# A tuned FFN-and-attention kernel: a new order of one tile's work on all five engines

## What is computed

```
xn  = layernorm(x)
# linear attention, 16 heads of 16
q, k, v = split(xn @ W_qkv.T + b_qkv);  q, k = elu(q) + 1, elu(k) + 1
kv  = sum_n k_n v_n ;  k1 = sum_n k_n
att = (q @ kv) / max(q . k1, 1e-6)
att = layernorm(att @ W_proj.T + b_proj) * gamma + beta + xn
# feed-forward with ternary weights, scales per output
h   = silu(xn @ w1.T * s1) * (xn @ w2.T * s2)       # 256 -> 1024
h   = gelu(h @ h1.T * t1)                           # 1024 -> 1024
h   = gelu(h @ h2.T * t2)                           # 1024 -> 1024
out = x + att + h @ w3.T * s3                       # 1024 -> 256
```

## Time and profile before

| what | value |
|---|---|
| median of 3 runs | 1734.03 us (1733.47 to 1736.09) |
| the profiled execution | 1730.4 us |
| its span in the profile | 1728.5 us |
| granted clock of TensorE, mean | 0.978 |
| busy: PE / DVE / ACT / POOL | 1562.2 / 1213.1 / 969.2 / 501.1 us |
| one tile of the loop | 102.1 us |
| from the start of the first tile's gate groups to that of the second's | 165.5 us |

### The profile page before, as it was taken

How to read it: one execution, slowest core, us unless ns; L and a number is a source line. 1 busy time by engine, 2 the same in 40 slices (tenths; PEclk the granted TensorE clock), 3 DMA queues, 4 the chain that set the end, 5 groups by cost and what they waited for, 6 DMA issues and landing times.

```text
span 1728.5 us, 32973 instructions
## 1 busy us (share of the span) xinstructions
PE 1562.2 (90%) x10956; PEld 1438.9 (83%) x10956; DVE 1213.1 (70%) x2083; ACT 969.2 (56%) x1745; POOL 501.1 (29%) x573
## 2 busy tenths in 40 slices
PE   6474999999999999999999999999999999999997
PEld 4474888888988888898888989888898888889897
DVE  3574686876868677685867768686685867768585
ACT  3243465655647465565755656565564656556463
POOL 3221150422314133240512314052231413323040
PEclk8697999999999999999999999999999999999999
DMA  6885255371735536173462626437172553717343
GB/s 229 316 325 187 92 205 182 109 255 51 263 106 182 195 112 234 57 252 138 140 232 91 228 89 227 162 116 254 52 260 98 195 186 113 243 43 261 129 159 132
DMA packets 84962, 298.15 MB, mean 172 GB/s; under 512 B 7232, under 2 KB 44224, under 8 KB 59584
## 3 DMA queue, kind: packets, MB, share of 16 engines
q0 software_dynamic: 37152, 238.04, 39.3%
q1 hardware_dynamic: 47344, 58.49, 10.0%
q10 hardware_dynamic: 432, 1.18, 0.2%
HBM read 280.91 MB, written 23.07 MB: 176 GB/s over the span
## 4 chain that ended last, share of the span: by engine, by line
PE 43%; DVE 20%; issue 16%; ACT 10%; DMA 4%; POOL 3%; DVEq 1%; SPq 0%; ACTq 0%; POOLq 0%
PE ps L830 19%; PE ps L859 7%; PE ps L804 5%; DVE partial_sums L1284 4%; PE ps L709 4%; DVE operands_a L1261 4%; PE ps L710 3%; PE ps L711 3%; DVE values_a L1253 3%; DVE operands_b L1261 2%; ACT operands_a L1008 2%; ACT values_out L1033 2%; ACT gate_ring L971 2%; POOL values_a L609 2%; DMA weight_set<-in_w_ffn 2%
## 5 line engine op out<-in xcount | busy, mean ns | idle before, releaser
L830 PE MATMUL ps<-operands_a,hidden_weights 128*128 128x256 f32 x5376 | 755.1, 286 | 61.6 <-DVE operands_a L1261 36.7
L830 PEld LDWEIGHTS ps<-operands_a,hidden_weights 128*128 128x128 f32 x5376 | 686.4, 191 | 88.1 <-DVE operands_a L1261 49.4
L830 PE MATMUL ps<-operands_b,hidden_weights 128*128 128x256 f32 x1792 | 298.2, 288 | 56.9 <-DVE partial_sums L1284 42.1
L830 PEld LDWEIGHTS ps<-operands_b,hidden_weights 128*128 128x128 f32 x1792 | 247.3, 191 | 69.6 <-DVE partial_sums L1284 45.8
L1284 DVE TENSOR_TENSOR partial_sums<-partial_sums,ps 128x512 f32<-128x512 f32 x320 | 214.3, 681 | 126.1 <-PE ps L830 125.5
L1261 DVE TENSOR_TENSOR operands_a<-values_a,operands_a 128x512 fp32r<-128x512 f32 x336 | 272.2, 825 | 41.9 <-ACT operands_a L996 22.3
L625 POOL DMA_DIRECT2D hidden_weights<-weight_blocks x252 | 138.0, 548 | 523.4 <-PE ps L830 510.6
L804 PE MATMUL ps<-xnT,w_ffn 128*128 128x512 f32 x1024 | 252.2, 401 | 15.3 <-DVE values_a L1253 15.3
L804 PEld LDWEIGHTS ps<-xnT,w_ffn 128*128 128x128 f32 x1024 | 191.7, 190 | 59.9 <-DVE values_a L1253 16.2
L1033 ACT ACTIVATE values_out<-partial_sums,vectors 128x256 f32<-128x256 f32 x192 | 86.9, 500 | 181.1 <-DVE partial_sums L1284 179.6
L1008 ACT ACTIVATE operands_a<-values_a 128x512 fp32r<-128x512 f32 x192 | 120.9, 630 | 107.8 <-POOL values_a L619 49.3
(11 more groups left out here) (112 smaller groups left out, 2083.2 us busy)
## 6 DMA issues: line engine op xcount, KB each, us to landing
hidden_weights<-weight_blocks POOLq DMA_DIRECT2D x192, 1024.0 KB, 5.6
hidden_weights<-weight_blocks POOLq DMA_DIRECT2D x64, 512.0 KB, 3.8
raw_weights<-weight_blocks SPq DMA_DIRECT2D x48, 272.0 KB, 5.5
x<-in_H SPq DMA_DIRECT2D x16, 512.0 KB, 5.1
weight_set<-in_w_ffn SPq DMA_DIRECT2D x16, 512.0 KB, 10.7
out_dram<-acc SPq DMA_DIRECT2D x32, 256.0 KB, 2.2
weight_blocks<-in_w_ffn SPq DMA_DIRECT2D x12, 512.0 KB, 10.6
weight_blocks<-weight_set SPq DMA_DIRECT2D x4, 1536.0 KB, 7.2
```

The source lines that it names most:

```text
L830: r = mm(bank[:, m * HT:(m + 1) * HT], ring_weights[:, place, 2 * g + j, m * P:(m + 1) * P], as_used(buf[:, j, slot[block_of_b], part, :]) ...
```

## The change

No operation is added or taken from the steady tile; the same instructions are issued in another order, and the waits are moved with them. The parts:

- **Product loops.** The chunk pair (g) is now the outer loop, then the part, then the bank's half (m), then the chunk.
- **Banks.** Set 0 and 2 use banks 4, 5, 0 in place of 0, 1, 4; sets 1 and 3 use 1, 2, 3 in place of 5, 2, 3. Only the wait conditions of the first products change.
- **PE.** The two `kv_sums` and the two first `apply_kv` come later among the gate groups; the attention projection (`proj_step`) comes after set 1's P1 and P6 instead of before them; in the first tile the next tile's transposes come after set 3's P6.
- **ACT, DVE, POOL.** Another order of conversions, sums, gelus, differences and refills. `keep_first` and the sums wait for the gelus that read `scratch` before them.
- **Weights.** All four sets are summed on DVE, set 0 in the prologue; the order is 0, 1, 2, 3; sets 0, 1, 2 use one area and set 3 a part of the other, once set 1's last product is done.
- **Prologue.** DVE no longer waits for PE's warm-up, SP no longer for the projection weights.

```
-BANKS = ((0, 1, 4), (5, 2, 3), (0, 1, 4), (5, 2, 3))
+BANKS = ((4, 5, 0), (1, 2, 3), (4, 5, 0), (1, 2, 3))
-    set_at = {0: z_at, 1: z_at, 2: ha_at + pair_bytes, 3: z_at}
+    set_at = {0: z_at, 1: z_at, 2: z_at, 3: ha_at + pair_bytes + o_bytes}
...
 SP, first tile
                         store_sums(1)
                         sp.wait_ge(s_stored[1], 32)
+                        load_set(2)
+                        copy_blocks(2)
+                        store_sums(2)
+                        sp.wait_ge(*prod.after(t, "1P4"))
                         load_set(3)
                         copy_blocks(3)
+                        load_x(t + 1, first)
                         store_sums(3)
-                        sp.wait_ge(s_stored[3], 32)
-                        load_x(t + 1, first)
 SP, prologue
-                sp.wait_ge(s_proj_raw, 16)
                 load_set(0)
                 copy_blocks(0)
-                sp.wait_ge(s_wproj, 2)
-                load_set(2)
                 store_sums(0)
-                copy_blocks(1)
-                store_sums(2)
                 sp.wait_ge(s_stored[0], 32)
                 load_set(1)
-                copy_blocks(2)
+                copy_blocks(1)
...
 PE, product
-                    for m in range(2):
-                        for g, group in enumerate(groups):
-                            buf, slot = operands(group)
-                            for part in range(2):
+                    for g, group in enumerate(groups):
+                        buf, slot = operands(group)
+                        for part in range(2):
+                            ...
+                            for m in range(2):
                                 for j in range(2):
 PE, body
                     product(t, 0, 3)
+
+                    product(t, 1, 1)
+                    product(t, 1, 6)
                     proj_step(t, 0)
                     proj_step(t, 1)
-
-                    product(t, 1, 1)
-                    product(t, 1, 6)
...
 ACT
             def keep_first(t, s):
                 act.wait_ge(*prod.after(t, f"{s}P1"))
+                if s > 0:
+                    act.wait_ge(*gelu.after(t, f"{s - 1}C21" if s % 2 else f"{s - 1}C12"))
...
 DVE
             def add_u(t, s):
                 dve.wait_ge(first_kept.sem, first_kept.at(t, s))
+                if s > 0:
+                    dve.wait_ge(*gelu.after(t, f"{s - 1}C12" if s % 2 else f"{s - 1}C21"))
                 sum_into(t, s, 6, 1, 0)
```

More of the change, by code:

```diff
@@ L652, in body @@
                         ln1(t + 1)
+                    if filling:
+                        if staging:
+                            pool.wait_ge(s_copied[2], 48)
+                        refill(t, 1, 0)
+                    t3(t, "H0")
                     if staging:
[L654 removed]
+                        inverse_root(t, 1, ln2_var, ln2_root)
+                        t4(t, "H0")
                         pool.wait_ge(s_stored[2], 32)
                     if filling:
[L657 removed]
@@ L841, in out_group @@
                     if n == 0:
-                        pe.wait_ge(*gelu.after(t, "2C11"))
+                        pe.wait_ge(*add.after(t, "2C12"))
                         if not full:
@@ L845, in out_group @@
                     else:
-                        pe.wait_ge(*add.after(t, "2C12"))
+                        pe.wait_ge(*gelu.after(t, "2C11"))
                     c1, c2 = (("C11", "C21"), ("C12", "C22"))[half]
@@ L880, in body @@
                 def body(t, more):
+                    staging = isinstance(t, int) and t == 0
                     gate_group(t, 0)
@@ L920, in body @@
                     product(t, 2, 7)
-                    if more:
+                    if more and not staging:
                         transposes(t + 1, 0)
@@ L928, in body @@
                     product(t, 3, 6)
+                    if staging:
+                        transposes(t + 1, 0)
+                        transposes(t + 1, 1)
                     product(t, 3, 2)
@@ L1505, in body @@
                         check_piece(t, 0)
+                    if checking:
                         check_piece(t, 1)
-                        check_piece(t, 2)
-                    if checking:
-                        check_piece(t, 3)
-                    add_u(t, 3)
-                    lo_of_output(t, 0, "C12")
-                    add_v(t, 3)
+                    if more:
+                        transposed_lo(t + 1, 1)
+                    add_v(t, 3)
+                    lo_of_output(t, 0, "C22")
@@ new lines, in body @@
+                    add_c22(t, 3)
+                    lo_of_output(t, 0, "C21")
+                    lo_of_output(t, 0, "C12")
+                    add_c12(t, 3)
+                    add_c21(t, 3)
+                    lo_of_output(t, 1, "C22")
+                    lo_of_output(t, 1, "C12")
+                    if checking:
+                        check_piece(t, 2)
+                    if more:
+                        put_ones(t + 1)
+                    lo_of_output(t, 0, "C11")
+                    lo_of_output(t, 1, "C21")
@@ L1513, in body @@
                     lo_of_output(t, 1, "C11")
                     ln2_apply(t)
-                    add_c22(t, 3)
-                    lo_of_output(t, 1, "C22")
-                    add_c12(t, 3)
-                    add_c21(t, 3)
-                    lo_of_output(t, 1, "C12")
-                    lo_of_output(t, 1, "C21")
                     if more:
+                        z_step(t + 1, 0)
+                        output(t, 0)
+                        z_step(t + 1, 1)
                         phi_q(t + 1, 0)
@@ L1544, in run @@
+                    output(t, 1)
                 over_tiles(dve, first, prologue, body)
```

302 lines of the change are left out of this document (152 added, 150 removed).

## The result

The changed kernel takes 1599.8 us (median of 4 runs, 1598.6 to 1600.2), the kernel before 1733.8 (4 runs beside it, 1732.3 to 1736.1): a ratio of 0.9225, 95% interval 0.9209 to 0.9241. The forecast was 1602, range 1578 to 1652. The profiled execution spans 1598.1 us, against 1728.5 before.

A forecast was written before the change was run, and what follows sets the result against it. PE was taken to set the time, its waiting being what can be won: 107 us from 15 tiles at 7.1 plus 25 in the first tile, 132 from 1730.4, gives 1598.4; with the median 3.6 above, 1602 us, range 1578 to 1652.

The forecast's parts named there:

- The signs: What would show it: loop tile 94 to 96 us, spacing 0.118 to 0.121, DVE without a 10 us stand.
- End of the block products: Loop tile: waits of 1.94 us behind `ln2_apply` and 0.97 behind `ln2_normalise` go; cover 1.2 us, cost nothing.
- Inside a product: Chunk pair outermost: high part wanted 0.48 us later, low 0.72, covering most of the 0.75 and 0.74 us waits.
- First products: Loop tile's first products: the 0.28 us wait goes, T1 of `G1` comes 0.4 late, cost 0.5 with the restart.
- Projection, border: Loop tile: projection moved behind two products, cover 0.5 us; border waits for `kv_sums` and a bank nothing, thinly covered.
- The sum of a tile: Loop tile: 93.7 us, plus 0.5 for T1 and 0.8 for three covers, makes 95.0, so 7.1 less.
- then it is a chain of DMAs: First tile after its gate phase: store, load, sum, store, refill; end at 170 to 172 us, gain 25.
- one of the loop: Last tile: taken for a loop tile, having the same gate phase and products, so 7.1 us less.
- Rival B: First tile: the chain of stores gives the gain back, ending it at 195; 1627 us, chance 0.13.
- A: Loop's first products: DVE, slowed by meetings with POOL, is pushed behind PE, 3.5 us a tile; 1654 us, chance 0.24.
- C: Products: changing bank half every second matmul costs per matmul; 1760 us at a spacing of 0.142; slower, chance 0.02.
- D: Loop: waits of another kind hold the same operands, the tile keeps its 102 us; 1709 us, chance 0.03.

The follow-up runs named there:

- e10: Kernel before with only `ln2_apply` moved late, behind the last piece of the last set: 1698.6 us, ratio 0.9797.
- e3: Changed kernel with `ln2_apply` put back ahead of `add_c22(t, 3)` on DVE: 1637.1 us.
- e11: Kernel before with `ln2_apply` late, `ln2_normalise` behind `keep_first(3)` and one output half, and products walked by chunk pair: 1693.3 us.
- e12: Kernel before with `ln2_apply` late and, on ACT, `keep_first(3)` ahead of the gelu of set 2's C12: 1687.5 us.
- e1: Changed kernel with the products walked by row half first again, all else kept: 1621.6 us.
- e2: Kernel before with only the change's product loops, chunk pair first: 1733.0 us, ratio 0.9999.
- e5: Changed kernel with the projection put back on PE ahead of set 1's first two products: 1661.7 us.
- e9: Changed kernel with the flag's matmul last on PE, POOL's two waits behind its differences, and set 1's sums in the first tile's gate phase: 1587.4 us.
- e6: Changed kernel, first tile only: set 0's four sums put between the `z_step`s on DVE, behind both `phi_q`: 1600.3 us.
- e7: Changed kernel, first tile only: POOL's waits for copied blocks of sets 2 and 3 put behind its differences: 1595.9 us, ratio 0.9198.
- e8: Changed kernel, last tile only: the check flag's matmul put behind the last output half on PE: 1593.2 us, ratio 0.9186.

## Why the prediction was right, and where it was wrong

**What bounds the kernel: right.** PE's waits are what was won, and in the loop nothing else became the bound. That the total fell within 2.2 us of the forecast is luck, as the table shows: the tile of the loop came out below the 94 to 97 us of the forecast's own range, and the first tile won 9.6 us, below its bounds of 15 and 38.

**The signs.** Those of the loop came: no wait at P2 and P4 of set 3, the largest left at set 0's second product, a spacing of 0.118. So did the first tile's gate phase without a gap and its three gaps for the ring. Three failed: the tile of 94 to 96 us (93.3), DVE without a stand of 10 us (20.9), and a second tile before 185 (187.6).

**End of the block products: one cause right, one wrong.** The 1.94 us wait did stand behind `ln2_apply`: 2.29 us a tile by e10, 2.19 by e3, the wait and a restart. The cover of 1.2 us held. The 0.97 us wait I put on `ln2_normalise`, because its 2.07 us stood last in front. It was a bystander: it ran while ACT had nothing else to do until C21 (e11). The gelu of C12 cost the time (0.82 by e12), and the change moved that gelu too, so the wait went as forecast, for a reason that was not the forecast's.

**Inside a product: right in kind, too small.** It is worth 1.76 us a tile (e1); the two waits that I named were 1.49, and I said most of them. But it comes only where other waits don't take it back (e2).

**First products: right.** 0.39 us, against 0.4.

**Projection, border: right, and thin.** Nothing waits there; e5 shows that the place of the projection carries 3.5 to 5 us once DVE's list is the new one. I had called this a cover of 0.5.

**The sum of a tile: 1.7 us too high.** 0.7 of it is the spacing: I took 0.120 from 64 matmuls without a bracket and had 448 of them. e1 shows 0.1184 under the old walk too, so the 1.6 ns are small stops of that stretch, not spacing. 0.8 is what I added for three thin covers, none of which cost anything. The last 0.2 I can't place.

**The first tile: the step "then it is a chain of DMAs" failed by its times, 15 us.** The chain is the one I named, and it fell behind stage by stage (us from the span's start):

| stage | forecast | measured |
|---|---|---|
| gate groups start | 29 | 34.0 |
| set 0 stored (next load issued) | 34 | 34.5 |
| set 1 loaded | 46 | 53.5 (e9) |
| set 1 stored | 69 | 73.8 |
| P6 of set 1 | 76 | 81.7 |
| set 2 stored | 103 | 106.4 |
| P5 of set 2 | 110 | 118.5 |
| set 3's sums begin | 121 | 132.2 |
| P6 of set 3 | 134 | 149.9 |
| second tile | 170 to 172 | 187.6 |

Four things: the gates started 5 us late, with DVE's sums of set 0 in front of what PE wanted, since their load landed at 22 us only (worth nothing in the end, e6); the load of set 1 took 19 us from its issue at 34.3 (e9) and not 12, and its sums then stood in DVE's list until 61.4 (2 to 5 us, e9); POOL's waits for copied blocks, 15 and 17 us long, which I did not follow at all (1 to 4 us, e7); and the sums of set 3 stand behind `add_u` of set 2, which I knew, so that each late refill delays the next stage whole. The last stage lost most, 16 us by P6 of set 3; from there on the forecast's 36 us were nearly right (37.7). No run parts the four cleanly. Rival B named this mechanism, and its sign (a second tile after 185) came true; the 1627 it gives did not, for the loop won more.

**The last tile: "one of the loop" failed, 11 us.** It has no next tile's work, and took 98.6 us before. Two parts failed. Up to the first output half it won 3.6 us and not 7.1: three waits are left there (1.99, 0.96 and 0.85 us; a tile of the loop has one of 0.39), which no experiment took up. From there on it lost 7.6, which I had put at nothing: the check of the last piece was moved behind `ln2_apply`, and PE's flag matmul waits for it ahead of an output half, 6.63 us against 1.35, and 2 more for the clock. e10 shows the same wait growing, and e8 wins 5 of it back.

**The rivals.** A: such meetings are in the trace, but by the mean durations below they cost less in the loop than before, and the tile was not pushed over 97.5. C: spacing 0.118; e1 and e2 both speak against a cost of alternating halves. D: each wait named went, whatever held it.

## What to carry to other kernels

An operation that stands last ahead of a late one need not be its cause: look whether the engine stood idle behind it, and for whom. The worth of one part of a reordering depends on which parts are in place: the walk gave 0 in the one kernel and 1.76 us a tile in the other. Cost the first and the last tile by their own lists, and where an in-order engine does staging work, ask in whose wake each piece stands, for that closes the loop of store, refill and product.

## What the runs showed of the hardware

**A stop can be longer than the gap that is printed.** Stops of 0.23 us in PE's row of products carried no bracket (e1); they show only as a group of four matmuls at 0.86 us beside others at 0.64.

**The clock falls behind short gaps, in some tiles.** Behind a wait of 1.94 us PE was granted 1.00 in one tile and 0.64 over 4 us in the next (e2); in the kernel before, 2 tiles of 14 were long (in one, the clock behind the same wait was 0.57 over 4 us), and in e10, without that wait, none. A long tile took 1.4 us more.

**VectorE stands while GpSimd subtracts.** In the first tile two subtractions of DVE (both operands in SBUF) took 3.81 us instead of 1.29, while POOL did two differences. DVE, then POOL:

```profile
57.69 3.81 DVE L1276 TENSOR_TENSOR operands_a<-values_a,operands_a 128x512 fp32r<-128x512 f32 x2
```

```profile
58.42 1.30 POOL L607 TENSOR_TENSOR values_a<-values_a 128x512 f32<-128x512 f32 x1
59.66 1.28 POOL L612 TENSOR_TENSOR values_a<-values_a 128x512 f32<-128x512 f32 x1
```

The 2.5 us more are what POOL's two took. In the prologue, where POOL no longer sums weights, DVE's q operation takes 0.68 us and not the 1.85 of the earlier trace rows. The Trainium skill, page "SBUF — State Buffer" (section on who interferes with whom), has it that the shared port pair is an exclusive lock, and that a DVE instruction with two SBUF inputs contends with a GpSimd one that reads SBUF; this trace agrees. What rival A missed is the count: in some two tiles of the loop (560 to 750 us) these subtractions take 763 ns (x42) and 687 ns (x14) on average, against 799 (x40) and 884 (x11) before. The new order loses less to them; that the meetings are fewer, and not shorter, is inferred.

**Copies inside DRAM land later than loads.** The page of the changed kernel, DMA issues, KB each and median us to landing:

```profile
weight_set<-in_w_ffn SPq DMA_DIRECT2D x16, 512.0 KB, 9.7
...
weight_blocks<-in_w_ffn SPq DMA_DIRECT2D x12, 512.0 KB, 14.7
weight_blocks<-weight_set SPq DMA_DIRECT2D x4, 1536.0 KB, 5.1
```

A copied block takes 14.7 us to land and a loaded one of the same size 9.7. The copies are issued behind the loads and run beside the ring's refill, so their own rate is not told by this. POOL's two long waits were for these.
